# Cross-attention and non-local block on one core: the second half's rows stay in fp32, the first half's output gets its own buffers, and the four engine orders are rewritten

## What is computed

```
def _L0_xattn_ref(x1, x2, Wq, bq, Wk, bk, Wv, bv):
    q = einsum('bcn,dc->bnd', x1, Wq) + bq          # 64 columns
    k = einsum('bcn,dc->bdn', x2, Wk) + bk
    v = einsum('bcn,dc->bdn', x2, Wv) + bv          # 512 channels
    attn = softmax(einsum('bnd,bdm->bnm', q, k), axis=2)
    return einsum('bcm,bnm->bcn', v, attn) + x1

def _L1_xattn_ref(x, x_2, ...):
    g_x, phi_x = conv1x1 of x_2;  theta_x = conv1x1 of x
    W = (theta_x^T phi_x) / 1024
    y = W g_x
    return batch_norm(w_w y + w_b) + x
```

## Time and profile before

| | |
|---|---|
| median of three runs | 1065.98 us |
| the profiled execution | 1065.61 us, of which 1063.8 us are its span |
| PE busy | 1042.0 us (98% of the span) |
| DVE busy | 722.1 us (68%) |
| ACT busy | 480.6 us (45%) |
| POOL busy | 280.5 us (26%) |
| DVE line 902 (`out`) | 64 operations, 58.7 us busy, mean 947 ns |
| DMA | 37.1% of 16 engines over the span |

### The profile page before, as it was taken

How to read it: one execution, slowest core, us unless ns; L and a number is a source line. 1 busy time by engine, 2 the same in 40 slices (tenths; PEclk the granted TensorE clock), 3 DMA queues, 4 the chain that set the end, 5 groups by cost and what they waited for, 6 DMA issues and landing times.

```text
span 1063.8 us, 13869 instructions
## 1 busy us (share of the span) xinstructions
PE 1042.0 (98%) x5104; PEld 850.5 (80%) x5104; DVE 722.1 (68%) x961; ACT 480.6 (45%) x810; POOL 280.5 (26%) x199
## 2 busy tenths in 40 slices
PE   6999999999999999999999999999999999999997
PEld 4688887888778887788877888778887888878886
DVE  6885388844888448884488745886368863788625
ACT  7753355434444345533545325453265532555411
POOL 1412261123501235012360123502244022440220
PEclk9999999999999999999999999999999999999999
DMA  6535251360513605236152351423424344243502
GB/s 237 169 78 143 107 198 43 75 217 27 195 42 73 215 29 197 50 89 198 41 178 58 106 175 64 155 72 106 160 70 149 80 112 146 81 140 78 136 23 79
DMA packets 80627, 122.06 MB, mean 115 GB/s; under 512 B 13104, under 2 KB 46384, under 8 KB 80560
## 3 DMA queue, kind: packets, MB, share of 16 engines
q1 hardware_dynamic: 80560, 121.17, 37.1%
HBM read 70.79 MB, written 16.78 MB: 82 GB/s over the span
## 4 chain that ended last, share of the span: by engine, by line
PE 88%; DVE 6%; DMA 3%; ACT 1%; issue 1%; SPq 0%; DVEq 0%; ACTq 0%
PE pG L573 33%; PE pG L472 13%; PE pG L584 8%; PE pG L480 6%; PE pG L513 4%; PE pG L487 4%; PE pT L594 3%; PE pS L525 3%; PE pT L525 2%; PE pG L594 2%; PE pM L552 2%; PE pM L561 2%; PE pS L451 2%; PE pT L462 2%; DVE xr L902 2%; DMA out_dram<-xr 1%
## 5 line engine op out<-in xcount | busy, mean ns | idle before, releaser
L573 PE MATMUL pG<-pt,vT 128*128 128x512 f32 x1536 | 352.9, 389 | 1.0 <-DVE pt L852 1.0
L573 PEld LDWEIGHTS pG<-pt,vT 128*128 128x128 f32 x1536 | 287.2, 188 | 60.2 <-issue 1.2
L472 PE MATMUL pG<-wv,x2s 128*128 128x512 f32 x768 | 182.9, 393 | 0.5 <-DVE vT L799 0.4
L881 DVE SCALAR_TENSOR_TENSOR xr<-pG,cl,xr 128x512 f32<-128x512 f32 x64 | 48.0, 751 | 189.2 <-PE pG L573 179.9
L931 POOL TENSOR_TENSOR xms<-xr,xms 128x512 fp32r<-128x512 f32 x64 | 87.7, 1370 | 319.6 <-ACT xms L726 319.6
L472 PEld LDWEIGHTS pG<-wv,x2s 128*128 128x128 f32 x768 | 142.1, 188 | 33.3 <-issue 3.3
L726 ACT ACTIVATE xms<-xr 128x512 fp32r<-128x512 f32 x64 | 40.3, 629 | 203.9 <-DVE xr L881 203.9
L852 DVE TENSOR_TENSOR pt<-mv,pt 128x512 fp32r<-128x512 f32 x128 | 89.8, 753 | 35.6 <-ACT pt L703 35.6
L923 POOL TENSOR_TENSOR x2Ts<-x2T_f,x2Ts 128x512 fp32r<-128x512 f32 x64 | 90.5, 1452 | 72.8 <-ACT x2Ts L672 72.7
L927 POOL TENSOR_TENSOR ys<-yf,ys 128x256 fp32r<-128x256 f32 x32 | 27.3, 854 | 306.1 <-ACT ys L694 306.1
L584 PE MATMUL pG<-xms,wth 128*128 128x512 f32 x384 | 90.1, 391 | 0.0
(11 more groups left out here) (112 smaller groups left out, 1420.9 us busy)
## 6 DMA issues: line engine op xcount, KB each, us to landing
mv<-tp SPq DMA_DIRECT2D x512, 64.0 KB, 2.0
st<-in_ctx_dram SPq DMA_DIRECT2D x32, 512.0 KB, 6.2
x2T_f<-in_ctx2T_dram SPq DMA_DIRECT2D x32, 512.0 KB, 6.2
xr<-in_x_dram SPq DMA_DIRECT2D x64, 256.0 KB, 3.4
out_dram<-xr SPq DMA_DIRECT2D x64, 256.0 KB, 2.8
st<-in_x_dram SPq DMA_DIRECT2D x29, 512.0 KB, 4.3
x_raw<-in_x_dram SPq DMA_DIRECT2D x3, 512.0 KB, 8.2
wv_f<-in_wvT_dram SPq DMA_DIRECT2D x4, 256.0 KB, 6.4
```

The costliest lines, as they stand in the source:

```text
L472: last = mm(bank, x2s[:, l, c, 128 * m:128 * m + 128], wv[:, r, c, :], start=(c == 0 and n == 0), stop=(c == 3 and n == 2))
L573: last = mm(bank, vT[:, l, m, 128 * c:128 * c + 128], pt(h)[:, r, m, :], start=(m == 0 and n == 0), stop=(m == 7 and n == 2))
```

## The change

1. **Second half.** `xr[c]` is kept in fp32 until the end. ACT adds the constant to it in place (new word `xc`, `Identity` with a bias, 128x512), after POOL has made the LO part. Then one DVE operation, `wy:1,c`, gives `xr[c] = gain * bank + xr[c]`, which is the output. The four `out:1,c` are gone, and SP's stores of half 1 wait for `wy:1,c`.
2. **First half.** `wy:0,c` and `out:c` build the output in new buffers `oh[c]`, which lie over the LO part of `xms0` that `wy` reads. `wy:1,c` no longer waits for the store of half 0; `k1` and `q1`, which lie over `oh`, wait for these stores instead of for `out:0,3`.
3. **x2T.** Its ACT step waits for the last `th` matmul instead of for `out:1`.
4. **Orders.** All strings but POOL's are new; POOL's words and SP's sequence stay.

```diff
...
                     for c in range(4):
-                        wait(eng, "oa", b, 4 * h + c)
-                        eng.dma_start(out[b, 128 * c:128 * c + 128, 512 * h:512 * h + 512], xr[c][:, :])\
-                           .then_inc(s_st[c], 16)
+                        dst = out[b, 128 * c:128 * c + 128, 512 * h:512 * h + 512]
+                        if h:
+                            wait_free(eng, b, G_WY + 4 + c)
+                            eng.dma_start(dst, xr[c][:, :]).then_inc(s_st[c], 16)
+                        else:
+                            wait(eng, "oa", b, c)
+                            eng.dma_start(dst, oh[c][:, :]).then_inc(s_so[c], 16)
...
+        oh = [at(f"oh{c}", [128, 512], F, rd + 4096 * c + 2048) for c in range(4)]
...
             def do_k(b):
                 wait(eng, "k", b, 1)
                 if b:
-                    wait(eng, "oa", b - 1, 3)
+                    for c in (0, 1):
+                        eng.wait_ge(s_so[c], 16 * b)
...
             def do_x2T(b, m):
                 eng.wait_ge(s_x2Td[m // 2], 16 * (b + 1))
                 if b:
-                    wait(eng, "oa", b - 1, 4 + m // 2)
+                    wait(eng, "g", b - 1, G_TH + 3)
...
+            def do_xc(b, c):
+                wait(eng, "xlo", b, 4 + c)
+                if b == 0:
+                    eng.wait_ge(s_cst, 4)
+                done(act(xr[c][:, :], xr[c][:, :], ACT.Identity, bias=cst(c)), "xc")
...
             def do_wy(b, h, c):
                 i = G_WY + 4 * h + c
                 wait(eng, "g", b, i)
-                if h == 0:
-                    wait(eng, "xlo", b, 4 + c)
+                if h:
+                    wait(eng, "xc", b, c)
+                    done(stt(out=xr[c][:, :], in0=bank_of(i), scalar=gain(c), in1=xr[c][:, :],
+                             op0=ALU.mult, op1=ALU.add), "gf")
                 else:
-                    eng.wait_ge(s_st[c], 16 * (2 * b + 1))
-                done(stt(out=xr[c][:, :], in0=bank_of(i), scalar=gain(c), in1=xms(h)[:, c, LO, :].bitcast(F),
-                         op0=ALU.mult, op1=ALU.add), "gf")
+                    done(stt(out=oh[c][:, :], in0=bank_of(i), scalar=gain(c), in1=xms0[:, c, LO, :].bitcast(F),
+                             op0=ALU.mult, op1=ALU.add), "gf")
...
 FIRST = dict(
...
     act=(
-        "w:0 x2:0 x2:1 xs:0 x2:2 x2:3 w:1 w:2 w:3 w:4 w:5 xs:1 xs:2 x1:0 x1:1 x1:2 v:0 x1:3 k xs:3 v:1 s k2 q "
+        "x2:0 w:0 xs:0 x2:1 x2:2 x2:3 xs:1 w:1 w:2 w:3 xs:2 w:4 xs:3 w:5 x1:0 x1:1 v:0 x1:2 s x1:3 k v:1 k2 q "
...
 LATER = dict(
     pe=(
-        "gs k:0 k:1 q:0 q:1 v:0 v:1 v:2 S:0 S:1 gt L:0 L:1 S:2 L:2 S:3 L:3 G:0 S:4 G:1 GT:0 G:2 G:3 v:3 S:5 v:4 "
+        "k:0 k:1 q:0 q:1 v:0 v:1 gs v:2 S:0 S:1 L:0 L:1 L:2 gt S:2 L:3 G:0 S:3 S:4 G:1 G:2 GT:0 G:3 v:3 v:4 v:5 "
```

More of the change, by code:

```diff
@@ L25 @@
     t1k=1, t1q=1, khi=1, qhi=1, vhi=8, exp=8, Thi=8, Ghi=4, Lhi=4, GThi=2, Yhi=4, shi=1, s_rowc=1, s_colc=1, mthi=1, Bhi=2,
-    xhi=8, thhi=4, x2hi=4, x1hi=4, x2Thi=8,
+    xhi=8, xc=4, thhi=4, x2hi=4, x1hi=4, x2Thi=8,
     kf=4, qf=2, klo=1, qlo=1, gf=36, mx=8, rec=8, norm=8, tr=8, Tlo=8, Glo=4, GTlo=2, slo=1, gsum=2, mtf=2, mtlo=1, Blo=2,
-    x2sum=4, x2lo=4, oa=8,
+    x2sum=4, x2lo=4, oa=4,
     x2Tlo=8, Ylo=4, xlo=8, x1lo=4,
@@ L236, in xattn_kernel @@
         s_st = [sem(f"s_st{i}") for i in range(4)]
+        s_so = [sem(f"s_so{i}") for i in range(4)]
         s_mv = [sem(f"s_mv{i}") for i in range(8)]
@@ L634, in do_q @@
                 if b:
-                    wait(eng, "oa", b - 1, 3)
+                    for c in (2, 3):
+                        eng.wait_ge(s_so[c], 16 * b)
                 done(act(q1[0:64, :], pT[64:128, :, :], ACT.Copy), "t1q")
@@ L735, in _ @@
             do = dict(w=do_w, x2=do_x2, xs=do_xs, x1=do_x1, k=do_k, q=do_q, k2=do_k2, q2=do_q2, v=do_v, S=do_S, L=do_L, G=do_G,
-                      GT=do_GT, Y=do_Y, x2T=do_x2T, s=do_s, T=do_T, gs=do_gs, gt=do_gt, mts=do_mts, B=do_B, PV=do_PV,
+                      GT=do_GT, Y=do_Y, x2T=do_x2T, s=do_s, T=do_T, gs=do_gs, gt=do_gt, mts=do_mts, B=do_B, xc=do_xc, PV=do_PV,
                       th=do_th)
@@ L892, in do_wy, with do_out @@
                 wait(eng, "g", b, i)
-                if h == 0:
-                    wait(eng, "xlo", b, 4 + c)
-                else:
-                    eng.wait_ge(s_st[c], 16 * (2 * b + 1))
-                done(stt(out=xr[c][:, :], in0=bank_of(i), scalar=gain(c), in1=xms(h)[:, c, LO, :].bitcast(F),
-                         op0=ALU.mult, op1=ALU.add), "gf")
-            def do_out(b, h, c):
-                wait_free(eng, b, G_WY + 4 * h + c)
-                done(stt(out=xr[c][:, :], in0=xr[c][:, :], scalar=cst(c), in1=xms(h)[:, c, HI, :].bitcast(F),
+                if h:
+                    wait(eng, "xc", b, c)
+                    done(stt(out=xr[c][:, :], in0=bank_of(i), scalar=gain(c), in1=xr[c][:, :],
+                             op0=ALU.mult, op1=ALU.add), "gf")
+                else:
+                    done(stt(out=oh[c][:, :], in0=bank_of(i), scalar=gain(c), in1=xms0[:, c, LO, :].bitcast(F),
+                             op0=ALU.mult, op1=ALU.add), "gf")
+            def do_out(b, c):
+                wait_free(eng, b, G_WY + c)
+                done(stt(out=oh[c][:, :], in0=oh[c][:, :], scalar=cst(c), in1=xms0[:, c, HI, :].bitcast(F),
                          op0=ALU.add, op1=ALU.add), "oa")
```

7 lines of the change are left out of this document (4 added, 3 removed), and 48 rows, old and new, of tables (act, dve, pe).

## The result

After the change the kernel takes 1073.45 us (median of four runs, 1070.72 to 1075.53); the kernel before, 1065.94 beside it. The ratio is 1.0074 with a 95% interval from 1.0045 to 1.0103: slower by about 7.5 us, where 1060.5 was forecast. It also lies above the stated range, which ended at 1069.5.

The account below looks back on a forecast made before the run. PE, busy 98% of the span, was taken as the bound. End -2.1, visits -3.4, starts -3.0, head +1.5 and middle +1.5 sum to -5.5 us: 1065.98 to 1060.5 us, range 1054.5 to 1069.5.

Parts of the forecast that it names:

- What bounds the kernel: PE, busy 98% of the span; an edit counts only where it removes PE's work or a wait of PE.
- Part 1, the end: Program's end: only wy:1,3 is left on DVE behind the last matmuls; -2.1 us, range -1.5 to -2.1.
- Part 2, fewer visits: PE's scores: one visit to 64-row S matmuls fewer per batch, eight in all; -3.4 us, range -2 to -3.4.
- the unit price: Cost on PE of one visit to the 64-row S matmuls between 128-row ones: 0.42 us.
- Part 3, the starts: Seven batch starts, first wy to S:0: waits of 4.2 us against 7.2; net -3.0 us, bounds -7.2 and +19.
- The slower rival: Batch starts: x1:3's low part past about 17.5, S:0 waits over 2 us, clock falls; +5.5, 1071.5 us; chance 16%.
- the moved sums: Batch starts: row sums xs:0, xs:1 behind the last th, so x block 1's load is issued at 2.0 us.
- Part 4, the head: Program's start: ACT's new order brings x blocks 1 to 3 about 1.1 us later; +1.5 us, range 0 to +3.
- Part 5, the middle: Middle of batches: later PV:0,2 and GT:1 on DVE cost 0.2 us a batch; +1.5 us, bounds -1.0 and 8 x 1.0.
- the room of 1.8 us: Middle of batches: DVE's PV:0,2 behind T:7 was to end 1.8 us before PE needs its bank for PV:1,0.

Follow-up runs that it names:

- e3: The kernel before with the new data path (xc, oh buffers, out:1 dropped) but its old orders: 1060.0 us, ratio 0.9941.
- e7: e3 with S:3 moved beside S:4 in PE's order of batches 1 to 7, DVE's order left old: 1069.66 us, ratio 1.0033.
- e5: The changed kernel with x2:3 of the next batch ahead of the last th on ACT and DVE: 1061.53 us, ratio 0.9964.
- e11: e9 with DVE's x2:3, and its s with it, put back into the wy stage behind out:2: 1067.57 us, ratio 1.0023.
- e8: e5 with the first batch's old orders up to its first S on PE, ACT and DVE: 1060.94 us, ratio 0.9961.
- e9: The changed kernel with old words around batch boundaries and in the head, new ones from S:0 to PV:1: 1055.41 us, ratio 0.9910.
- e13: The changed kernel with v:0 ahead of x2T:2 and q on ACT and ahead of q on DVE, batches 1 to 7: 1076.26 us, ratio 1.0098.
- e10: The changed kernel with only ACT's x2:3 moved ahead of the last th, DVE's left in place: 1069.14 us, ratio 1.0033.
- e12: The changed kernel with x2T:0 put behind k and s on ACT in batches 1 to 7: 1071.23 us, ratio 1.0055.
- e2: The changed kernel with q1 ahead of x2T:2 on ACT in the later batches: 1066.74 us, ratio 1.0018.

## Why the prediction was wrong

**What bounds the kernel**: right. The DVE operations taken away bought the end and little else (e3), and PE's batch starts decided.

**Part 1, the end**: right to a tenth of a microsecond, 2.1.

**Part 2, fewer visits**: the unit price was right (0.43 measured in e7, 0.42 from the earlier trace rows). PE's edit alone lost 9.7 us in e7, so the saving needed DVE's new order with it.

**Part 3, the starts**: here the prediction failed, +10.5 for -3.0. Its path began well: the low part of `x1:3` at 16.3 (15.5 measured), POOL and DVE stretching each other as the earlier trace rows showed. The Trainium skill (SBUF — State Buffer, Who interferes with whom) has it as a rule that a VectorE operation with two SBUF inputs contends with a GpSimd operation that reads SBUF. The trace agrees, with 8.90 us for POOL's three and 3.43 and 2.90 for DVE's two. Three steps behind that failed.
- *Load 1 of x2T "lands some 4.3 later".* It took 5.87, and 4.7 to 7.5 in six of the seven starts. The 4.3 was the x loads' time, taken in the belief that the queue ahead was empty. But load 0, issued at 13.6 (677.55), was still under way: the sum followed the meeting of DVE and POOL to the low part of `x1:3`, and not to `out:3`, the store behind it and load 0 behind that. Where load 0 left at 11.4, load 1 took 3.7. The `x2T` loads take 6.2 us to land on the page of after, as they did before; that row was there to be used.
- *Only `klo` was followed to `S:0`.* The path was `qf`, `qhi`, `qlo`, `klo`: 28.0. Between them and PE stands `v:2`, which needs the bank of `v:0`, and the low part of `v:0` stands on DVE behind `qf`. `v:2` started at 26.34 at the boundary shown, and `S:0` is 2.96 behind it. In before `q1` started at 19.3 to 20.7 and `v:2` was seldom held; the earlier trace rows showed this wait, 1.3 us for `vT` in two batches, and I added it to what could be won without asking who would lengthen it.
- *"No drop of the clock (an assumption)".* With waits of 3.33 and 1.75 us it fell twice, 4.3 us.

The slower rival had the right kind of sum (1071.5) and named the low part of `x1:3`. But its condition was not met, 15.5 against "past about 17.5", and it is not what decided: the seventh start has 15.6 and no wait for `v:2`. That its 1071.5 lies near the measured time is luck in part. Its 16% were too few.

What neither it nor the forecast had is what stands behind `x2:3`. I had looked at the moved sums, which seem to cost little (e5 against e3), and treated `x2:3` as an operation that takes time on DVE and POOL only. Behind it on DVE stands `out:3`, which SP's last store and load 0 wait for: that made the loss in after. And ACT's next copy of the same buffer, `xs:3`, waits for it, with everything behind on ACT: that made the loss in e11. e5 and e11 show the place of `x2:3` as the larger part of the loss, 12 us from either side. e5 alone does not part these paths; the seventh start of after does.

**Part 4, the head**: +1.1 for +1.5 in the span; its worth in time is open (e8).

**Part 5, the middle**: parts 2 and 5 together gave -4.4 for -1.9, of which 1.5 is the slow clock that stood behind before's 2.33 us wait and that the prediction counts in part 3; so -2.9 is what compares with -1.9. The bank of `PV` cost 2.3 us in three waits, for the 1.0 of `pt` that went. Two of them, 0.43 and 0.51, are the case weighed there: DVE runs `PV:0,2` only behind `T:7`'s low half, and the room of 1.8 us worked out from the second batch is gone in these two. The third, 1.40, is in the first batch, where DVE itself waited 2.1 us for a load of `xr`.

## What to carry to other kernels

Follow every operand of the late instruction: here `S:0` stood behind a projection whose bank was freed by a third engine's queue, and a path that is right for one operand is only a lower bound. When an operation is moved, ask what the operations behind it on its own engine release elsewhere (here a store, and with it the next load in SP's order), and who must not touch its buffer until it has read it. Strings for four engines are one object: change a data path with the old orders first (e3), then take the new orders stretch by stretch (e9); with all new words the kernel lost 7.5 us, and with the new ones from `S:0` to `PV:1` alone it won 9.4.

## What the runs showed of the hardware

- Between the program's head and its last `wy` stage the fourteen traces have 20 waits of PE of 1.75 to 3.33 us. Behind 13 of them the granted clock fell to 0.50, 1.2 GHz (before 2.33; after 3.33 and 1.75; five of e13's seven); behind 7, of 1.91 to 2.26 us (e8, e10, e11, e12, e13), it did not. It never fell behind a shorter one: 1.73 us in after, and in e2 and e3, where no wait at a start was over 1.5, the granted clock was 1.000 on the mean. So the length of the wait alone does not settle it in that range. A fall cost 1.5 to 1.7 us beyond the wait, the one in after's first start 2.6, so several short waits are cheaper than one long: e2 with 9.9 us of waits is 6.7 us faster than after with 9.6.
- Load 1 of `x2T` (512 KB) took 4.7 to 7.5 us to land in the 74 starts of all traces where it was issued less than 2.5 us behind load 0, and 3.5 to 5.2, with a median of 3.6, in the 24 where it was issued 2.9 us or more behind. The stores around the loads differ too between these starts, so the distance is not shown to be the only cause.
- DVE's `wy:1` (one operand in PSUM, one in SBUF) ran at its own 0.7 us beside POOL's low parts, while `x2:3` and `out`, with both operands in SBUF, took 3.43 and 2.90. The Trainium skill (SBUF — State Buffer, Who interferes with whom) says that a VectorE operation with at most one SBUF input, outside its 2-port modes, does not contend with GpSimd, and the trace agrees. But no engine was waiting for DVE there.
